# Shared expert units with their low parts on GpSimd, a single-pass table, and a reordered start of Mamba

## The chip, the cores and the metric

The kernel runs on one core of a Trainium2 chip. Time is the device time of one execution in microseconds (us). The engines are TensorE (PE, with its weight loads as PEld), VectorE (DVE), ScalarE (ACT), GpSimd (POOL) and SyncE (SP), which here only issues DMAs.

## The reference

A float32 stack over 4 x 1024 tokens of width 128. Each line normalises x and adds a layer's output:

```python
x = x + 0.5 * moe(layernorm(x))       # 8 experts, 2 per token, one shared
x = x + mamba(layernorm(x))           # forward and reversed selective scan
x = x + 0.5 * moe(layernorm(x))
x = x + 0.5 * ternary_ffn(layernorm(x))
x = x + attention(layernorm(x))       # causal, 16 heads
x = x + 0.5 * ternary_ffn(layernorm(x))
```

The expert layer and the core of the Mamba layer are:

```python
gates = softmax(relu(xf @ Wr1 + br1) @ Wr2 + br2)
tg, ti = top_k(gates, 2); tg = softmax(tg / 2)
out = silu(xf @ Ws1 + bs1) @ Ws2 + bs2
for e in range(8):
    h = silu(xf @ We1[e] + be1[e]) @ We2[e] + be2[e]
    out = out + sum(tg * (ti == e), -1)[:, None] * h
...
h = exp(dt * A) * h + (dt * x) * B_t      # per step, 16 states
y = sum(h * C_t) + x * D
```

## The kernel before, in words

The six layers run one after the other, in program order: experts (3 to 281 us), Mamba (284 to 1310), experts again (about 1316 to 1586), ternary, attention, ternary. The tokens lie in SBUF as x, in 8 blocks of 512 (BLK).

**Matmul precision.** A float32 product is made of three matmuls in the fp32r format: a value is split into a high part (the fp32r copy, by ACT or DVE) and a low part (value minus high), and high x high, low x high and high x low are summed in PSUM. Some matmuls (the table and positions, below) have plain float32 operands.

**Expert layer (`moe_ffn`).** First come norm and router for all eight blocks. Then the work goes in 31 *units*: 8 shared ones (SH, one per block, with the shared weights), then 23 jobs of 512 gathered rows with one expert's weights each. A unit u is: `up` on PE, four chunks k of 128 hidden channels; ACT writes each chunk as raw (Silu, float32) and for k = 0 to 2 again as hh (Silu, fp32r); DVE's `low(u, k)` makes hl = raw - hh, and for k = 3 also hh by a copy; `down` on PE from hh and hl; ACT evicts; PE transposes (`out_T`); DVE's `take` adds the rows to x (shared units) or copies them to yt, which SP stores. raw has one buffer a chunk, hh and hl two.

Beside the shared units DVE carries the routing, in an order written out by hand in its unit loop: `gate_top` ahead of the loop, `gate_second` (second choice, ends with s_M, a copy to spare) after (0, 1), `counts`, `places`, `split_places` (ends with s_dst, another copy to spare) up to (1, 1). PE's `positions` sits between. Then `hot(q)`, q = 0 to 15, each four scaled one-hot tiles `oha` (128x96) and one tile of one-hots `ohb` (128x512, in pool8, which it shares with the normalised rows xn), placed by `GROUPS`; PE multiplies them into a *table* in PSUM (`table`, 64 float32 matmuls), which says what token stands in each of the gathered places. `experts` makes the expert of each job, `indices` (after unit 5) turns the table into gidx. POOL waits for gidx and gathers: `gather(j)` is four indirect DMAs of rows, `weights(j)` one of a job's weights. POOL's order is: power for the gates (tt), weights 0 to 2, gathers 0 to 2, then gather(j + 2), weights(j + 2) for each job. DVE's `weights` (after unit 2) turns tt into the gates wab, which are used in the next layer when the experts' rows are added.

**Mamba (`mamba`).** The scan goes in 16 blocks b of 16 slots v, with a block -1 that only prepares. `uses_of(b)` says which use of the one PSUM tile O lies in which slot: T transposes a chunk's rows, x is half a convolution (12 fp32r matmuls), xp the projection to B, C and dt, dt its second product, z the gate. `silus_of` places ACT's silus. In each slot PE broadcasts a row of B (`rows`), DVE makes a product u x B over 128x1024 (L1645) and two scans (L1621), POOL two products H x C (L1757), and POOL makes dt and u of the next block, 3 to 6 slots after each dt use. Before that, POOL fetches the expert layer's rows back into a ring (`fetch`, one indirect DMA each, 8 a block), ACT weighs them (`weigh`), DVE adds them (`returned`) and takes statistics; `root(n)` on POOL makes the reciprocal root and `normalize` on ACT the rows of a chunk.

## Time and profile before

| | |
|---|---|
| median of 3 runs | 2830.28 us (2826.9 to 2831.55) |
| the profiled execution | 2828.44 us |
| its span | 2826.6 us |
| granted TensorE clock, mean | 0.949 |
| PE busy | 2464.1 us (87%) |
| DVE busy | 2216.3 us (78%) |
| ACT busy | 1698.0 us (60%) |
| POOL busy | 1431.2 us (51%) |

These shares are means over layers with different limits. The slices below (40 equal ones of 70.7 us, busy share in tenths) show the first expert layer in slices 1 to 4, Mamba in 5 to 19, the second expert layer in 20 to 22:

```profile
PE   7998387878888898887899599979999999997999
DVE  7998478989999999998899556458877777755444
POOL 2474688888888888885177460023233323310000
```

In Mamba DVE and POOL are the busiest, in the expert layers PE and DVE.

### The profile page before, as it was taken

What the parts mean: (1) busy time and instruction counts of PE and PEld (TensorE: products, weight loads), DVE (VectorE), ACT (ScalarE), POOL (GpSimd) and SP (SyncE); (2) the same over time, 40 slices, a digit from 0 to 9 for tenths busy, and PEclk for the clock granted to TensorE, in tenths of its full rate; (3) what the DMA queues carried; (4) which work ended last, traced back from release to release, by engine and by line L of the source; (5) the groups of instructions that cost most, each with busy time, mean ns of one, the idle gap of its engine ahead of it and who ended that gap; (6) DMA issues with size and microseconds to landing.
All of it is one profiled execution on the core that took longest, in us unless ns stands there. A gap on an engine that the chain in (4) does not pass through costs nothing. (4 is left out here: it accounts for less than half of the span.)

```text
span 2826.6 us, 35819 instructions
## 1 busy us (share of the span) xinstructions
PE 2464.1 (87%) x10648; PEld 1570.2 (56%) x10648; DVE 2216.3 (78%) x4293; ACT 1698.0 (60%) x2969; POOL 1431.2 (51%) x1482
## 2 busy tenths in 40 slices
PE   7998387878888898887899599979999999997999
PEld 5876243333333344324777378855555555646887
DVE  7998478989999999998899556458877777755444
ACT  3676465556666666652477355535776767764555
POOL 2474688888888888885177460023233323310000
PEclk9999598999999999999999799989999999998999
DMA  2256222222222222222056410000000000001000
GB/s 76 64 163 117 84 68 67 74 69 73 68 75 73 75 75 75 72 78 73 24 129 146 98 49 2 1 16 1 1 1 1 2 1 1 1 1 42 8 8 15
DMA packets 99497, 146.07 MB, mean 52 GB/s; under 512 B 13036, under 2 KB 50540, under 8 KB 99124
## 3 DMA queue, kind: packets, MB, share of 16 engines
q1 hardware_dynamic: 82196, 98.60, 11.7%
q0 software_dynamic: 16608, 44.78, 7.4%
q8 instruction: 83, 1.36, 0.2%
q14 instruction: 98, 0.80, 0.1%
q10 hardware_dynamic: 512, 0.53, 0.1%
HBM read 124.98 MB, written 18.87 MB: 51 GB/s over the span
## 5 line engine op out<-in xcount | busy, mean ns | idle before, releaser
L1757 POOL TENSOR_TENSOR a_hc<-a_H,a_cb 128x512 f32<-128x512 f32 x512 | 619.3, 1231 | 135.1 <-DVE a_H L1621 128.1
L1413 PE MATMUL a_Y<-a_hc,ident 128*128 128x512 f32 x1024 | 539.4, 637 | 54.4 <-POOL a_hc L1757 45.9
L2113 ACT ACTIVATE a_pt<-a_W 128x512 f32<-128x512 f32 (+3 forms) x768 | 345.8, 496 | 201.7 <-PE a_W L2013 198.1
L1539 ACT ACTIVATE a_dA<-a_dt,a_aneg 128x512 f32<-128x512 f32 x512 | 342.6, 714 | 193.9 <-POOL a_dt L1776 103.8
L1413 PEld LDWEIGHTS a_Y<-a_hc,ident 128*128 128x128 f32 x1024 | 183.6, 197 | 306.9 <-POOL a_hc L1757 211.8
L1645 DVE TENSOR_TENSOR a_BX<-a_u,a_BX 128x1024 f32<-128x1024 f32 x256 | 308.4, 1210 | 43.8 <-PE a_BX L1347 22.0
L1621 DVE TENSOR_TENSOR_SCAN a_H<-a_dA,a_H,a_BX 128x512 f32<-128x512 f32 x256 | 312.2, 1262 | 2.5 <-ACT a_dA L1539 2.5
L2336 POOL TENSOR_SCALAR_AFFINE_SELECT a_pt<-a_pt 128x512 f32<-128x512 f32 x128 | 91.3, 713 | 421.9 <-ACT a_pt L2113 421.9
L1621 DVE TENSOR_TENSOR_SCAN a_H<-a_dA,a_BX 128x512 f32<-128x512 f32 x256 | 296.5, 1201 | 1.0 <-POOL a_hc L1757 1.0
L2199 DVE CUSTOM_DVE_ANT_0 a_masked<-a_W,a_mask 128x384 f32<-128x384 f32 (+3 forms) x512 | 231.9, 486 | 78.8 <-PE a_W L2000 76.8
L2013 PE MATMUL a_W<-a_Q,a_K 128*128 128x512 f32 (+3 forms) x768 | 283.8, 385 | 1.7 <-ACT a_pt L2113 1.6
L2000 PE MATMUL a_W<-a_K,a_Q 128*128 128x512 f32 (+3 forms) x768 | 268.6, 364 | 8.5 <-POOL a_K L2345 3.9
L1347 PE MATMUL a_BX<-a_bcs,a_sel 128*128 128x512 f32 x256 | 174.4, 682 | 96.8 <-DVE a_H L1621 82.9
L722 POOL DMA_INDIRECT m_xg<-m_xrows,m_gidx x184 | 190.8, 1037 | 120.9 <-DVE m_didx L606 65.4
L1053 DVE TENSOR_TENSOR t_hl<-t_raw,t_hh 128x512 fp32r<-128x512 f32 x128 | 87.4, 691 | 182.1 <-ACT t_hh L954 182.1
L2013 PEld LDWEIGHTS a_W<-a_Q,a_K 128*128 128x128 f32 x768 | 145.8, 191 | 138.5 <-ACT a_pt L2113 90.2
L2202 DVE TENSOR_REDUCE a_mx<-a_W 128x1 f32<-128x512 f32 x256 | 166.4, 678 | 46.9 <-PE a_W L2000 46.8
L448 ACT ACTIVATE m_raw<-m_U,m_wg 128x512 f32<-128x512 f32 x248 | 173.9, 702 | 45.9 <-PE m_U L336 33.3
L849 PE MATMUL t_U<-t_hh,t_wh 128*128 128x512 f32 x512 | 201.4, 393 | 0.0
L851 PE MATMUL t_U<-t_hl,t_wh 128*128 128x512 f32 x512 | 199.6, 390 | 0.0
L850 PE MATMUL t_U<-t_hh,t_wl 128*128 128x512 f32 x512 | 199.3, 389 | 0.0
L953 ACT ACTIVATE t_raw<-t_U,t_scal 128x512 f32<-128x512 f32 x128 | 88.1, 688 | 166.6 <-PE t_U L851 166.6
(324 smaller groups left out, 5462.8 us busy)
## 6 DMA issues: line engine op xcount, KB each, us to landing
a_cb<-a_crow SPq DMA_DIRECT2D x256, 256.0 KB, 3.3
m_orows<-m_yt SPq DMA_DIRECT2D x46, 256.0 KB, 3.2
t_wst<-ternary_w SPq DMA_DIRECT2D x22, 256.0 KB, 2.7
m_xrows<-m_pool SPq DMA_DIRECT2D x16, 256.0 KB, 2.3
m_xg<-m_xrows,m_gidx POOLq DMA_INDIRECT x184, 3.5
out<-x SPq DMA_DIRECT2D x8, 256.0 KB, 2.3
m_wg<-moe_ws SPq DMA_DIRECT2D x2, 516.0 KB, 4.6
a_hc<-mamba_conv_rows SPq DMA_DIRECT2D x1, 1024.0 KB, 5.1
```

The lines of the kernel that those rows point to most:

```text
L849: pe.matmul(out, wh[:, piece, c], rhs_h, start=start, stop=False)
L850: pe.matmul(out, wl[:, piece, c], rhs_h, start=False, stop=False)
L851: return pe.matmul(out, wh[:, piece, c], rhs_l, start=False, stop=stop)
L1413: pe.matmul(Y[:, h, :], ident[:], hc[:, g % HCRING, :], start=False, stop=v == NS - 1).then_inc(s_y, 1)
L1539: act.activation(dA[:, G % ARING, :], dt[:, b % 2, h, :], ACT.Exp, scale=aneg[:, d, h, v:v + 1]).then_inc(s_dA, 1)
L1621: dve.tensor_tensor_scan(out, a, bb, init, ALU.mult, ALU.add).then_inc(s_scan, 1)
L1645: dve.tensor_tensor(both_banks(Q), u[:, b % 2, :, :], BX[:, row_bank(Q), :].unsqueeze(1).broadcast_to([P, HALF, BLK]), ALU.mult).then_inc( ...
L1757: pool.tensor_tensor(hc[:, G % HCRING, :], H[:, s, span], cb[:, v % RING, :], ALU.mult).then_inc(s_hc, 1)
L2000: pe.matmul(W[:, s % 3, 0:cols], Q[:, g, tile(t)], K[:, g * GH + j, c * BLK:c * BLK + cols], start=True, stop=True).then_inc(s_S, 1)
L2013: pe.matmul(W[:, 3 + u % 3, 0:BLK - r * P], K[:, g * GH + j, tile(kt)], Q[:, g, c * BLK + r * P:(c + 1) * BLK], start=True, stop=True).the ...
L2113: act.activation(pt[:, u % PR, 0:BLK - r * P], W[:, 3 + u % 3, 0:BLK - r * P], ACT.Exp).then_inc(s_exp, 1)
L2199: dve.tensor_tensor_reduce(masked[:, s % 3, 0:cols], W[:, s % 3, 0:cols], mask[:, BLK - cols:], 1.0, LEAST, ALU.add, ALU.max, dst).then_in ...
```

## The change

In the expert layer, POOL makes the low parts of shared units 0 to 5 (`NPL`), and for k = 3 the high part too, with semaphores of their own (s_hp, s_h3); `low_done` says who signals which. The tables' operands are fp32r: oha, the one-hot tiles (now `slots`, five buffers apart from xn), both, and the constants for `positions`, which ACT copies to `sums`. `table` is one fp32r matmul for each of the 64. `GROUPS` starts at (2, 0) instead of (1, 2) and ends at (5, 1); `indices` follows at (6, 1) and is one step and a cast, since the table's values are now stored as token - 2048. Gate scratch tiles are reused. On POOL the order is low parts of units 0 to 4, weights 0 to 2, low parts of unit 5, gathers 0 to 2, then the power for the gates, then the rest; DVE's `weights` moves from unit 2 to unit 10.

In Mamba, chunk 1's transpose and convolution go from block 0 to block -1 (slots 10, 12, 14), its projection and dt to earlier slots of block 0; its silu from slot 4 to 2; ACT weighs ring block 1 at (-1, 3) and normalises chunk 1 at (-1, 8); POOL fetches 12 rows ahead of the first root, then 4, clears H, fetches 4.

```diff
-        pool8 = sb("pool8", [P, 8, BLK])
-        xn = pool8[:, 0:NXN, :]
-        oha = sb("oha", [P, NOA, TPB, HOT])
+        xn = sb("xn", [P, NXN, BLK])
+        slots = sb("slots", [P, NOB, BLK], F32R)
+        oha = sb("oha", [P, NOA, TPB, HOT], F32R)
...
+        both = sb("both", [P, TILES, E], F32R)
+        sums = sb("sums", [P, 2 * P], F32R)
...
-        GROUPS = {(1, 2): (0, 1), (1, 3): (1, 3), (2, 0): (3, 4), (2, 1): (4, 5), (2, 2): (5, 6), (2, 3): (6, 8),
-                  (3, 0): (8, 9), (3, 1): (9, 10), (3, 2): (10, 11), (3, 3): (11, 13),
-                  (4, 0): (13, 14), (4, 1): (14, 15), (4, 2): (15, 16)}
-        TABLE_DONE = 5
+        GROUPS = {(2, 0): (0, 1), (2, 1): (1, 2), (2, 2): (2, 3), (2, 3): (3, 4), (3, 0): (4, 5), (3, 1): (5, 6),
+                  (3, 2): (6, 7), (3, 3): (7, 9), (4, 0): (9, 10), (4, 1): (10, 11), (4, 2): (11, 12),
+                  (4, 3): (12, 14), (5, 0): (14, 15), (5, 1): (15, 16)}
+        TABLE_DONE = (6, 1)
+        NPL = 6
+
+        def low_done(u, k):
+
+            return (s_hp, KC * u + k + 1) if u < NPL else (s_hl, KC * (u - NPL) + k + 1)
         def ohb(q):
-            return pool8[:, (NXN + q) % NOB, :]
+            return slots[:, q % NOB, :]
...
-                        pe.wait_ge(s_hl, KC * u + k + 1)
+                        pe.wait_ge(*low_done(u, k))
...
-                    pe.matmul(T[:, 0:E * TILES], C["tri"], m, start=True, stop=True)
-                    pe.matmul(T[:, E * TILES:], C["ones"], m, start=True, stop=True).then_inc(s_pos, 1)
+                    pe.matmul(T[:, 0:E * TILES], sums[:, 0:P], m, start=True, stop=True)
+                    pe.matmul(T[:, E * TILES:], sums[:, P:], m, start=True, stop=True).then_inc(s_pos, 1)
...
-                pe.wait_ge(s_consts, 16)
+                pe.wait_ge(s_sums, 1)
...
-                        wait(act, s_hl, KC * (u - 1) + k + 1)
+                        if u:
+                            act.wait_ge(*low_done(u - 1, k))
...
+                        act.wait_ge(s_consts, 16)
+                        act.activation(sums[:], cst[:, 0:2 * P], ACT.Copy).then_inc(s_sums, 1)
...
-                    if NOB - NXN <= q < NOB:
-                        dve.wait_ge(s_xst[q - NOB + NXN], 16 * (SH // NXN))
...
-                    val = T[:, 0:COLS]
-                    step(dve.tensor_scalar(g1_[:], val, float(TOKENS) + 0.5, float(TOKENS), ALU.is_ge, ALU.mult))
-                    step(dve.scalar_tensor_tensor(g2_[:], val, -1.0, g1_[:], ALU.add, ALU.subtract))
-                    step(dve.tensor_scalar(gidx[:], g2_[:], 0.0, None, ALU.max))
+                    step(dve.tensor_scalar(gidx[:], T[:, 0:COLS], float(TOKENS // 2), None, ALU.add))
...
-                        if u < UNITS:
+                        if NPL <= u < UNITS:
                             low(u, k)
...
+                        if (u, k) == TABLE_DONE:
+                            indices()
+                    if u == SH + 2:
                         weights()
-                    if u == TABLE_DONE:
-                        indices()
...
+                def low(u, k):
+                    if k < KC - 1:
+                        pool.wait_ge(s_hh, 3 * u + k + 1)
+                        if k == 0:
+                            wait(pool, s_dn, u - 1)
+                    else:
+                        pool.wait_ge(s_raw, KC * (u + 1))
+                        pool.tensor_scalar(hh[:, u % 2, k, :], raw[:, k, :], 1.0, 1.0, ALU.mult, ALU.mult)\
+                            .then_inc(s_h3, 1)
+                        pool.wait_ge(s_h3, u + 1)
+                    pool.tensor_tensor(hl[:, u % 2, k, :], raw[:, k, :], hh[:, u % 2, k, :].bitcast(F32),
+                                       ALU.subtract).then_inc(s_hp, 1)
+
+                for u in range(NPL):
+                    for k in range(KC):
+                        low(u, k)
+                    if u == NPL - 2:
+                        pool.wait_ge(s_ej, 1)
+                        for j in range(NWG - 1):
+                            weights(j)
                 pool.wait_ge(s_consts, 16)
-                pool.wait_ge(s_dd, 1)
-                pool.tensor_tensor(tt[:], root_e[:], dd[:], ALU.pow).then_inc(s_tt, 1)
-                pool.wait_ge(s_ej, 1)
-                for j in range(NWG - 1):
-                    weights(j)
                 pool.wait_ge(s_idx, 1)
                 for i in range(NXN):
                     pool.wait_ge(s_xst[i], 16 * (SH // NXN))
                 for j in range(NXG):
                     gather(j)
+                pool.wait_ge(s_dd, 1)
+                pool.tensor_tensor(tt[:], root_e[:], dd[:], ALU.pow).then_inc(s_tt, 1)
...
-                    7: ("dt", 0, 0), 9: ("dt", 1, 0)}
+                    7: ("dt", 0, 0), 9: ("dt", 1, 0), 10: ("T", 0, 1), 12: ("x", 0, 1), 14: ("x", 1, 1)}
         if b == 0:
-            return {0: ("T", 0, 1), 1: ("x", 0, 1), 2: ("x", 1, 1), 5: ("xp", 0, 1), 6: ("x", 0, 2),
-                    7: ("dt", 0, 1), 8: ("x", 1, 2), 9: ("dt", 1, 1), 10: ("z", 0, 0), 11: ("z", 1, 0),
+            return {3: ("xp", 0, 1), 5: ("dt", 0, 1), 6: ("x", 0, 2), 7: ("dt", 1, 1), 8: ("x", 1, 2),
+                    10: ("z", 0, 0), 11: ("z", 1, 0),
...
-            return {4: (1, None), 12: (2, 0)}
+            return {2: (1, None), 12: (2, 0)}
...
-                        if (b, v) == (-1, 7):
+                        if (b, v) == (-1, 3):
                             back.weigh(act, ring, 1, 0, s_weighed)
                             back.weigh(act, ring, 1, 1, s_weighed)
-                        if (b, v) == (-1, 12):
+                        if (b, v) == (-1, 8):
                             normalize(1)
...
-                fetch(2 * TPB)
+                fetch(2 * TPB + 4)
+                root(0)
+                fetch(4)
                 pool.memset(H[:], 0.0).then_inc(s_cst, 1)
-                root(0)
-                fetch(2 * TPB + 4)
+                fetch(4)
                 root(1)
...
-    val = (np.arange(2)[:, None] * TOKENS + TILE * P).reshape(1, -1) + p + 1
+    val = np.tile(TILE * P, 2)[None] + p - TOKENS // 2
```

## Rows read from the trace of the kernel before

**Rows 1.** Windows by stage: us, each engine's busy time, PEclk, DMA share, GB/s.

```profile
40.00:112.00 72.00, 60.40 (x319) 50.13 (x319) 65.01 (x173) 37.61 (x60) 15.01 (x10) 0.95 0.10 27
112.00:220.00 108.00, 107.45 (x525) 85.58 (x524) 106.31 (x179) 86.88 (x148) 83.26 (x82) 1.00 0.54 142
...
338.00:412.00 74.00, 57.96 (x154) 30.63 (x154) 56.83 (x52) 48.74 (x81) 62.71 (x56) 0.87 0.24 70
```

**Rows 2.** Timeline, 44 to 64 us, DVE: start, length, instruction, [idle before <-releaser].

```profile
49.49 0.15 DVE L535 COPY m_spare<-m_both 128x1 f32<-128x1 f32 x1
...
59.70 0.15 DVE L575 COPY m_spare<-m_dmod 128x1 f32<-128x1 f32 x1
60.37 1.04 DVE L589 TENSOR_SCALAR m_oha<-m_cst,m_dbase 128x96 f32<-128x96 f32 x4
61.32 0.68 DVE L594 TENSOR_TENSOR m_pool<-m_cst,m_dmod 128x512 f32<-128x512 f32 x1
```

**Rows 3.** The same timeline, PE.

```profile
62.06 2.02 PE L389 MATMUL m_T<-m_oha,m_pool 128*128 128x96 f32 x8 [6.43 <-DVE m_pool L594]
```

**Rows 4.** Timeline around 104 us, DVE and then POOL.

```profile
104.38 0.20 DVE L606 CAST m_didx<-m_dest 128x64 uint32<-128x64 f32 x1
...
104.84 0.95 POOL L722 DMA_INDIRECT m_xg<-m_xrows,m_gidx  x1 [32.71 <-DVE m_didx L606]
```

**Rows 5.** Groups by shape, POOL: xcount | busy us, mean ns | idle before.

```profile
L1757 POOL TENSOR_TENSOR a_hc<-a_H,a_cb 128x512 f32<-128x512 f32 x512 | 619.3, 1231 | 135.1 <-DVE a_H L1621 128.1 <-PE a_Y L1413 6.0
...
L104 POOL DMA_INDIRECT a_ring<-m_orows,m_didx x64 | 64.0, 1000 | 14.0 <-issue 11.1 <-POOL a_pads L1716 0.5 <-PE a_Y L1413 0.5
...
L2345 POOL TENSOR_SCALAR a_K<-a_stk,a_heads 128x512 fp32r<-128x512 f32 x128 | 88.1, 704 | 9.2 <-DVE a_stk L2265 9.2
```

**Rows 6.** Timelines at about 298, 435 and 652 us, DVE and POOL.

```profile
298.27 0.69 DVE L122 TENSOR_TENSOR x<-x,a_ring 128x512 f32<-128x512 f32 x1 [1.14 <-ACT a_ring L114]
...
435.27 4.94 DVE L122 TENSOR_TENSOR x<-x,a_ring 128x512 f32<-128x512 f32 x2
...
435.93 2.50 POOL L1757 TENSOR_TENSOR a_hc<-a_H,a_cb 128x512 f32<-128x512 f32 x2
...
438.39 1.26 POOL L1776 TENSOR_TENSOR a_dt<-a_rl,a_um 128x512 f32<-128x512 f32 x1
...
652.69 2.55 DVE L122 TENSOR_TENSOR x<-x,a_ring 128x512 f32<-128x512 f32 x2
...
651.73 2.95 POOL L1757 TENSOR_TENSOR a_hc<-a_H,a_cb 128x512 f32<-128x512 f32 x2 [0.24 <-DVE a_H L1621]
```

**Rows 7.** Expert-stage timelines; DMA issues (us to landing); waits, 112 to 282.

```profile
49.27 5.48 POOL L735 TENSOR_TENSOR m_tt<-m_root_e,m_dd 128x32 f32<-128x32 f32 x1 [16.20 <-DVE m_dd L532]
...
125.85 0.94 POOL L713 DMA_INDIRECT m_wg<-moe_we,m_widx  x1 [0.30 <-issue]
...
132.50 0.46 DVE L639 CAST m_w1h<-m_wg 128x512 fp32r<-128x512 f32 x1
...
m_wg<-moe_we,m_widx POOLq DMA_INDIRECT x46, 4.3
...
DVE m_w1h L639 <- DMA m_wg<-moe_we,m_widx: 5.7, 4, 2.5
```

**Rows 8.** Timeline, DVE, Mamba's first two blocks.

```profile
337.68 2.36 DVE L1645 TENSOR_TENSOR a_BX<-a_u,a_BX 128x1024 f32<-128x1024 f32 x2
...
355.26 1.23 DVE L1645 TENSOR_TENSOR a_BX<-a_u,a_BX 128x1024 f32<-128x1024 f32 x1 [5.69 <-PE a_BX L1347]
...
411.62 2.36 DVE L1645 TENSOR_TENSOR a_BX<-a_u,a_BX 128x1024 f32<-128x1024 f32 x2 [10.87 <-POOL a_u L1770]
```

**Rows 9.** Timelines, PE at 346 us and POOL at 366 us.

```profile
346.26 0.79 PE L1365 MATMUL a_O<-a_xh,a_wch 128*128 128x512 f32 x1 [3.14 <-DVE a_xl L1665]
...
348.99 0.63 PE L1365 MATMUL a_O<-a_xh,a_wch 128*128 128x512 f32 x1
...
366.71 2.20 POOL L1757 TENSOR_TENSOR a_hc<-a_H,a_cb 128x512 f32<-128x512 f32 x2
```

More of the change, by code:

```diff
@@ L174, in moe_ffn @@
             at += n
-        NWG, NXG, NYT, NXN, NOB, NOA = 4, 3, 3, 4, 8, 5
+        NWG, NXG, NYT, NXN, NOB, NOA = 4, 3, 3, 4, 5, 5
         wg = sb("wg", [P, NWG, ROW])
@@ L197, in moe_ffn @@
         g1 = lambda n: sb(n, [P, TILES])
-        sh, ex, gt, eq, cc, oh1, gm, oh2, both, pr1, pr2 = map(g8, (
-            "sh", "ex", "gt", "eq", "cc", "oh1", "gm", "oh2", "both", "pr1", "pr2"))
-        eq2, cc2 = g8("eq2"), g8("cc2")
+        sh, ex, gt, eq, cc, oh1, gm, oh2, pr1, pr2 = map(g8, (
+            "sh", "ex", "gt", "eq", "cc", "oh1", "gm", "oh2", "pr1", "pr2"))
+        both = sb("both", [P, TILES, E], F32R)
+        sums = sb("sums", [P, 2 * P], F32R)
         mx, sm, rs, top1, cm, top2, cm2, dd, tt, t1, w0 = map(g1, (
@@ L211, in moe_ffn @@
         widx = sb("widx", [P, JOBS], U32)
-        g1_, g2_ = (sb(n, [P, COLS]) for n in ("g1", "g2"))
         gidx = sb("gidx", [P, COLS], U32)
@@ L226, in moe_ffn @@
         s_wsh, s_wsl = sem("wsh"), sem("wsl")
+        s_sums = sem("sums")
         s_mv, s_ve, s_rstd, s_xn = sem("mv"), sem("ve"), sem("rstd"), sem("xn")
@@ L233, in moe_ffn @@
         s_up, s_raw, s_hh, s_hl = sem("up"), sem("raw"), sem("hh"), sem("hl")
+        s_hp, s_h3 = sem("hp"), sem("h3")
         s_dn, s_ye, s_yT, s_yo = sem("dn"), sem("ye"), sem("yT"), sem("yo")
@@ L530, in gate_second @@
                     step(dve.scalar_tensor_tensor(gm[:], oh1[:], -2.0, gt[:], ALU.mult, ALU.add))
-                    first_of_equals(gm, top2, eq2, cc2, cm2, oh2)
+                    first_of_equals(gm, top2, eq, cc, cm2, oh2)
                     dve.tensor_tensor(dd[:], top2[:], top1[:], ALU.subtract).then_inc(s_dd, 1)
@@ L534, in gate_second @@
                     ch.join()
-                    dve.tensor_copy(spare[:], both[:, 0, 0:1]).then_inc(s_M, 1)
+                    dve.tensor_copy(spare[:], both[:, 0, 0:1].bitcast(F32)).then_inc(s_M, 1)
                 def weights():
@@ L693, in _ @@
                                 experts()
-                    if u == 2:
+                        if (u, k) == TABLE_DONE:
+                            indices()
+                    if u == SH + 2:
                         weights()
-                    if u == TABLE_DONE:
-                        indices()
             @block.gpsimd
```

## The prediction

> **What bounds the kernel now.** I read the windows by stage first, then the timelines of VectorE (DVE), GpSimd (POOL), TensorE (PE) and ScalarE (ACT) in the three stretches that the diff touches, and last, for prices, the grouped instructions. The diff acts in two expert stages, near 40 and near 1346 us, which in the timeline are copies of each other 1305.7 us apart, and once in the first blocks of Mamba. What lies outside only moves with them.
>
> In the shared part of an expert stage (40 to 112 us) DVE is busy 65.0 of 72 us and POOL 15.0 [rows 1]. DVE carries the router, then the destinations, then sixteen pairs of one-hot tiles, with the low parts of the hidden rows between them. PE idles 6.43 us for the first pair, and starts cold after it [rows 3]. The part ends in a handover: the indices are written at 104.38, POOL's first gather starts at 104.84, and PE transposes the gathered rows some 8 us later [rows 4]. From 112 to 220 us DVE is busy 106.3 of 108 us, and POOL issues without a pause in the same rhythm, 6.65 us for one unit (weights of job 3 issued at 125.85, DVE's cast that is in step with them a unit later at 132.50) [rows 1, 7]. Near its end the stage waits for the gathered weights, 5.7 us in four waits [rows 7]. So what a shorter shared part is worth is the shift of the first gather, and whatever delays POOL behind it comes off again.
>
> In Mamba DVE multiplies and scans. The first product starts at 337.68; then DVE idles 5.69 us before 355.26, since PE is busy with convolution matmuls of the second block, and 10.87 us before 411.62, since POOL hasn't finished that block's u [rows 8].
>
> **Experts: what leaves DVE.** 24 low parts (a DVE operation of this size is 0.69 long and starts the next some 0.60 later) and six casts (0.46 for one) [rows 6, 7] are 17.1 us of DVE per stage, some 14.5 of them ahead of the handover. Without any other effect my step-by-step schedule gives: s_M at 48.4 instead of 49.5, destinations at 56.5 instead of 59.7 [rows 2], then four or five pairs a unit at 1.57 us (1.04 and 0.68 us overlapping a little) [rows 2], which PE (28 matmuls a unit, 60.40 us for 319 [rows 1], so some 5.8 us a unit with the residual rows, and the table between) follows in 7.6 to 8.1 us; gather at 90.3. That is 14.5 us earlier per stage, the upper bound.
>
> **Experts: what POOL takes.** A two-input POOL operation of 128x512 took 1.23 us, a one-input one to fp32r 0.70 [rows 5]; so 4 x 1.23 + 0.70 = 5.6 us a unit. It is shorter than the 7.6 us pace: POOL as such isn't the bound. But the rows show that DVE and POOL hold each other up. DVE's sum of two SBUF tiles takes 0.69 us alone; two of them took 4.94 us while POOL did three two-input operations (435.93 to 439.65) [rows 5, 6], and 2.55 us against two, of which POOL's own second was stretched, 2.95 for both [rows 6]. In the first case DVE waited until POOL paused, in the second they alternated. DVE's work here is of that kind: nine of the twelve steps of the second choice, most of the places, and the one-hot tile of each pair (iota and dmod both in SBUF).
>
> The Trainium skill, page "SBUF — State Buffer", section "Who interferes with whom", says that a VectorE instruction with two SBUF inputs contends with a GpSimd instruction that reads SBUF, and that the second to issue blocks entirely until the first is done. By that rule 14.5 us can't be had; the trace agrees in that 0.69 became 4.2 for one, but it also shows a wait across several operations, which the rule, read as one instruction, doesn't give.
>
> With alternation, step by step: POOL's first low part runs from 44.0 to 45.25, and each two-input step of DVE then waits for the one in progress, about 0.7 us; the second choice ends at 54.0 instead of 49.5. PE has idled 6 us by then and starts cold [rows 3]. Counts, places and split, with POOL in the way until about 58.5, give destinations at 64.6 (59.7 before). From here the pairs run with fewer neighbours: a unit of five pairs and the residual add is 5 x 1.57 + 0.6 = 8.5 us plus 1.2 to 2 us of waits, about 10, where it was 11.5 to 12.3 before. The sixteenth pair is in the table at 99.8. The indices now come one unit later in the order, after out_T of unit 4, so 102.6; the first gather at 102.9. Gain 1.95 us per stage, between -8 (DVE waits for POOL's pauses throughout; see the rivals) and 14.5. I take alternation, since the stretch in which POOL's operands come in one at a time from ACT resembles the second case more.
>
> **Experts: the order on POOL.** The power for the gates, 5.48 us on POOL [rows 7], moves from 49.27, where POOL had nothing else to do, to behind the first twelve gathers. Queued behind it are gather 3, weights 3 and all later ones, with no pause in which to recover. Weights 3 were issued at 125.85, landed 4.3 us later at the median and are cast at 132.50 [rows 7], so 2.3 us of the 5.8 (with the issue) are covered: 3.5 us lost there. At the end, where the weights come last, the whole 5.8 counts, less what POOL catches up. I take 4.3, bounds 0 and 5.8. Its price is the same if the first gather moves, because everything behind it moves along. Weights 0 to 2 go behind the fourth unit's low parts, 3.8 us of issue, hidden since no one needs them before the handover. The table's cheaper passes and the positions' are on PE, which waits for DVE; at nothing, at most a microsecond if DVE weren't last. The new wait for sums on PE and ACT's copy lie 15 us ahead of use; the freed xst waits had been satisfied. Per stage: 1.95 - 4.3 = -2.35, so 4.7 us slower in both.
>
> **Mamba.** Moved ahead of block 0: the transpose and both convolution halves of chunk 1; inside it, the projection from slot 5 to 3 and dt from 7, 9 to 5, 7. Fetches go from 8 + 12 around root(0) to 12 + 4 + 4, so ring 1 is landed at about 312 and is weighed in ACT's gap after its first silu; sums and setup end on DVE at 323.3. But ACT's normalize(1) now stands ahead of dt and waits for root(1) until 324.0. u of block 0 ends at 338.1 (337.6 before). Then PE does 24 convolution matmuls, the first twelve cold (such a run started at 346.26 and its seventh at 348.99, 0.455 us apiece, about 5.3 in all) [rows 9], and the first row broadcasts stand behind them: first product at 342.4 instead of 337.7, 4.7 us late. The 5.69 us and one xl (0.6) are gone from block 0, so by the sixth product DVE is 1.7 to 1.9 ahead. The end of block 0 goes by POOL: from 366.71 [rows 9] it works through v = 5 to 15: 11 pairs of products at 2.46 or less, six fetches at 1.00 [rows 5], eight steps to dt and u and two bcs at 1.26 [rows 6], 45.7 us, so until about 412, which fits DVE's start at 411.62 [rows 8]. Moved two slots earlier, v = 14 and 15 (two pairs of products, a fetch, a bcs: 4.9 + 1.0 + 1.3, 7.3 us with the gap between) no longer lie ahead of u: 7.3 + 1.9 = 9.2 us gained. These 7.3 us remain as POOL's backlog in block 1; it idled 11 us there before. I keep 9.2; bounds 3 and 14 (PE cold for all 24 and backlog paid; POOL not last).
>
> **Sum.** 9.2 - 4.7 = 4.5 us faster against the profiled execution's 2828.4 us (span 2826.6), 2823.9; that execution lies 1.8 under the median of the runs shown, so 2825.8 for a median, rounded to 2826.
>
> **Rivals.** (1) Starvation, slower: DVE waits for POOL's pauses, as in the first of the two cases. Then s_M waits until POOL has run out of units 0 and 1, 58.6; destinations 67.5; a unit of five pairs 12.4 us; first gather 112.8, 8 us later than now. It decides as soon as POOL's next operand is ready before its operation ends in the stretch 44 to 58. For it: ACT delivers a chunk about every 1.2 us (an estimate: two passes of its own a chunk, and PE at 5.8 us for four), POOL needs 1.23. Against: the two stretched pairs. Per stage -8 - 4.3: 24.6 in both, with 9.2 back, 15.4 slower: 2846. (2) Contention light: gather at about 92 to 96; 2 x (10.5 - 4.3) + 9.2 = 21.6 faster: 2809; the full bound, 14.5, gives 2801. For it: between chained steps of DVE there are gaps. Against: both of the overlaps in [rows 6] were stretched. (3) Mamba gives only 3, or the late start costs more, with alternation: 2832.
>
> **Chances.** Alternation 0.38, starvation 0.24, light contention 0.26, weak Mamba 0.12. A measurement of this kernel tells 0.2%, 5.7 us, from no change. Alternation itself straddles that bound on the fast side (4.5 us), so I share it: 0.17 faster, 0.16 same, 0.05 slower. With the rest: faster 0.17 + 0.26 + 0.02 = 0.45; same 0.16 + 0.02 + 0.05 = 0.23; slower 0.05 + 0.22 + 0.05 = 0.32. Range 2802 to 2846; the likeliest case's own is 2818 to 2834.
>
> **What would show it.** In the changed profile: the spare copy behind the second choice near 54 (48.4: no contention; 58.6: starvation); two-input DVE operations of 1 us and more beside POOL's, and whether one ever waits through two; the first gather near 102.9; an idle DVE before the cast of w1h at job 3 of 3 to 4 us; stage end to follow. In Mamba, the first product near 342, no idle before the fourth, and block 1's first near 402. I am wrong if DVE's waits beside POOL are rare, or if DVE is starved.

## The result

The changed kernel takes 2851.82 us (median of 5 runs, 2842.25 to 2854.85) against 2830.28 (2826.9 to 2834.07): 1.0069 times the time before, 95% interval 1.0055 to 1.0083, so 0.7% slower. The forecast was 2826, range 2802 to 2846.

| | before | changed |
|---|---|---|
| profiled execution | 2828.44 us | 2854.85 us |
| its span | 2826.6 us | 2853.1 us |
| DVE busy | 2216.3 us | 2223.4 us |
| POOL busy | 1431.2 us | 1506.3 us |

DVE was to lose 34 us of work (17 a stage), yet its busy time rose by 7: the trace counts an instruction as busy while POOL holds it up (the rows of L599 below). That is the first thing to see. The windows of the changed kernel, same stretches and columns as [rows 1]:

```profile
40.00:112.00 72.00, 53.70 (x224) 42.88 (x223) 64.34 (x129) 32.63 (x53) 40.29 (x33) 0.81 0.07 23
112.00:220.00 108.00, 102.09 (x485) 81.52 (x484) 96.21 (x167) 79.86 (x136) 82.17 (x77) 0.97 0.50 124
```

From 40 to 112 us DVE is busy as long as before with 129 instructions instead of 173, and PE has done 224 matmuls where it had done 319, at a granted clock of 0.81 in the mean. Of the 95 that are missing 66 are no lag: the table and the positions are now one pass each (66 matmuls instead of 132). The other 29 are.

Where the 26.5 us of span lie, from the timelines of both. "Router" is the reduction m_mx on DVE (40.0 us in both), "last tile" the start of the sixteenth one-hot tile, "first gather" POOL's first m_xg, "end" the last job's copy m_yt on DVE, all in us:

| first expert stage | before | changed | later by |
|---|---|---|---|
| router to last tile | 57.3 | 66.2 | 8.9 |
| last tile to first gather | 7.5 | 8.9 | 1.4 |
| first gather to first job's copy | 29.4 | 32.0 | 2.6 |
| first to last job's copy | 146.0 | 149.0 | 3.0 |
| sum: router to end | 240.2 | 256.0 | 15.8 |

The second stage goes from 240.4 to 256.5, 16.1 longer. Mamba gives 6.1 back (end of stage to the start of DVE's last product: 1022.0, now 1015.9), the rest is 0.6 longer: 15.8 + 16.1 - 6.1 + 0.6 = 26.4 (0.1 is lost in rounding).

The timeline of the changed kernel's DVE shows how (start, length, instruction; x4 is four in a row, "..." stands for rows left out):

```profile
39.97 0.42 DVE L530 TENSOR_REDUCE m_mx<-m_T 128x32 f32<-128x256 f32 x1 [3.02 <-PE m_T L320]
...
52.07 0.15 DVE L545 COPY m_spare<-m_both 128x1 f32<-128x1 f32 x1
...
64.29 0.15 DVE L585 COPY m_spare<-m_dmod 128x1 f32<-128x1 f32 x1
64.36 2.90 DVE L599 TENSOR_SCALAR m_oha<-m_cst,m_dbase 128x96 fp32r<-128x96 f32 x4
...
83.90 4.14 DVE L599 TENSOR_SCALAR m_oha<-m_cst,m_dbase 128x96 fp32r<-128x96 f32 x4
87.96 0.68 DVE L602 TENSOR_TENSOR m_slots<-m_cst,m_dmod 128x512 fp32r<-128x512 f32 x1
...
95.11 4.33 DVE L599 TENSOR_SCALAR m_oha<-m_cst,m_dbase 128x96 fp32r<-128x96 f32 x4
...
106.19 0.69 DVE L602 TENSOR_TENSOR m_slots<-m_cst,m_dmod 128x512 fp32r<-128x512 f32 x1
111.07 0.69 DVE L621 TENSOR_TENSOR m_hl<-m_raw,m_hh 128x512 fp32r<-128x512 f32 x1 [4.19 <-ACT m_hh L460]
...
114.13 0.20 DVE L611 CAST m_didx<-m_dest 128x64 uint32<-128x64 f32 x1
```

POOL in the same timeline:

```profile
84.16 3.81 POOL L748 TENSOR_TENSOR m_hl<-m_raw,m_hh 128x512 fp32r<-128x512 f32 x3 [6.37 <-ACT m_hh L460]
...
115.08 1.09 POOL L727 DMA_INDIRECT m_xg<-m_xrows,m_gidx  x1 [13.93 <-DVE m_didx L611]
```

Four small operations take 1.04 us when nobody disturbs them [rows 2]. At 83.90 they take 4.14 us, exactly beside three subtractions of POOL. Over the whole kernel the groups say the same (columns as in [rows 5]); first before, then changed:

```profile
L589 DVE TENSOR_SCALAR m_oha<-m_cst,m_dbase 128x96 f32<-128x96 f32 x128 | 33.6, 326 | 0.0
```

```profile
L748 POOL TENSOR_TENSOR m_hl<-m_raw,m_hh 128x512 fp32r<-128x512 f32 x48 | 65.6, 1386 | 54.4 <-ACT m_hh L460 53.2
...
L599 DVE TENSOR_SCALAR m_oha<-m_cst,m_dbase 128x96 fp32r<-128x96 f32 x128 | 59.1, 524 | 0.0
```

The 128 one-input operations of the tables cost 25.5 us more, 12.8 a stage. The 32 two-input tiles behind them cost nothing: all but one have the length of before (shortest, median and longest in ns):

```profile
L602 DVE TENSOR_TENSOR m_slots<-m_cst,m_dmod x32: 677/680/1136, 67.2 to 1422.3; 128x512 fp32r<-128x512 f32 x32
```

Added up instruction by instruction against the shortest of its kind before, the first stage's DVE operations up to the last tile are 21.4 us longer, 15.8 of it in one-input operations.

### The profile page after: what moved, and what is told of

It is laid out like the page before. It is cut to its first block and busy times, and to the rows that moved or that the text cites. A ratio compares the mean times of both kernels' runs of the same rounds, so it can differ in the third digit from the quotient of the medians.

```text
span 2853.1 us, 35545 instructions
## 1 busy us (share of the span) xinstructions
PE 2465.8 (86%) x10516; PEld 1565.2 (55%) x10516; DVE 2223.4 (78%) x4229; ACT 1698.5 (60%) x2971; POOL 1506.3 (53%) x1542
## 5 line engine op out<-in xcount | busy, mean ns | idle before, releaser
L1369 PE MATMUL a_BX<-a_bcs,a_sel 128*128 128x512 f32 x256 | 174.1, 681 | 85.7 <-DVE a_H L1643 84.1
L1075 DVE TENSOR_TENSOR t_hl<-t_raw,t_hh 128x512 fp32r<-128x512 f32 x128 | 87.5, 691 | 181.7 <-ACT t_hh L976 181.6
L727 POOL DMA_INDIRECT m_xg<-m_xrows,m_gidx x184 | 179.0, 973 | 82.2 <-issue 54.3
L456 ACT ACTIVATE m_raw<-m_U,m_wg 128x512 f32<-128x512 f32 x248 | 174.3, 704 | 44.1 <-PE m_U L343 34.7
## 6 DMA issues: line engine op xcount, KB each, us to landing
a_cb<-a_crow SPq DMA_DIRECT2D x256, 256.0 KB, 3.2
m_orows<-m_yt SPq DMA_DIRECT2D x46, 256.0 KB, 4.7
t_wst<-ternary_w SPq DMA_DIRECT2D x22, 256.0 KB, 2.8
m_xrows<-m_xn SPq DMA_DIRECT2D x16, 256.0 KB, 2.3
out<-x SPq DMA_DIRECT2D x8, 256.0 KB, 2.3
```

## The experiments

Each ratio below is against the kernel before, run beside it. The experiments fall into four sets: A (mamba_alone, pow_back, npl_zero, early_indices), in which the kernel before took 2911.79 us, B (free_pool, probe, table_only, all_good) with 2828.68, C (pow_late, pow_back_2, npl_two, all_good_2) with 2829.24, and D (changed_again, npl_zero_2, all_good_3) with 2901.68. In A and D, the long sets, the part from the first gather to the stage's end was 198 to 209 us instead of 174 to 183 in every kernel. What makes a set long is open: the record has chip number 12 for B and for D. Totals are therefore compared within a set only, and ratios of different sets with care: npl_zero and npl_zero_2 are one kernel, and came to 0.9999 and 0.9959, with intervals that do not overlap. Up to the last tile the changed kernel agrees between a short and a long set within 1.4 us (66.2 and 66.8, 65.9 and 65.4), in Mamba within 0.7; its first gather scatters more (75.1 and 74.8, 71.1 and 74.2), so that a difference of less than 4 us there says little. Numbers from the timelines, in us, first and second stage:

| kernel | router to last tile | router to first gather | first gather to end | end to last product of Mamba |
|---|---|---|---|---|
| before | 57.3, 57.4 | 64.8, 64.9 | 175.4, 175.5 | 1022.0 |
| changed | 66.2, 66.8 | 75.1, 74.8 | 180.9, 181.7 | 1015.9 |
| npl_zero | 59.2, 59.1 | 67.5, 64.9 | 204.5, 207.3 (long set) | 1016.3 |
| npl_two | 59.6, 59.6 | 68.1, 66.9 | 180.9, 181.7 | 1016.0 |
| free_pool | 44.4, 45.4 | 51.4, 52.4 | 182.5, 180.7 | 1014.6 |
| pow_back_2 | 65.8, 65.5 | 74.6, 71.5 | 177.6, 178.0 | 1016.1 |
| table_only | 57.3, 57.4 | 65.5, 65.2 | 174.0, 174.1 | 1021.7 |
| all_good | 57.4, 57.4 | 64.2, 63.3 | 174.3, 173.8 | 1013.1 |
| pow_late | 56.3, 56.3 | 63.1, 64.6 | 181.3, 181.7 | 1013.3 |
| all_good_2 | 57.4, 57.4 | 62.5, 63.8 | 179.5, 177.0 | 1009.3 |

### The probe: which operations hold each other up

Behind the end of the kernel before, eight each of seven kinds of DVE operation, four times: alone, beside POOL subtractions (two SBUF inputs), beside POOL's one-input operation, beside POOL memsets.

```diff
+for part in range(4):                        # DVE; POOL runs 76 or 90 operations beside parts 1 to 3
+    for i in range(8): dve.tensor_scalar(o1[:, i, :], sa[:, 0:96], sc[:, 0:1], sc[:, 1:2], ALU.is_equal, ALU.mult)
+    for i in range(8): dve.tensor_tensor(o2[:, i, :], sa[:], sb_[:], ALU.is_equal)
+    for i in range(8): dve.tensor_tensor(o3[:, i, :], Z[:], sb_[:], ALU.subtract)      # Z in PSUM
+    ...
```

> The kernel before, and behind its end a probe: eight each of seven kinds of DVE operation (one-input with two per-partition scalars from SBUF 128x96; two SBUF inputs 128x512; PSUM and SBUF 128x512; one-input from PSUM 128x96; reduction 128x256; cast 128x512; scalar_tensor_tensor from PSUM and SBUF), first alone, then beside an unbroken row of POOL subtractions 128x512, then beside one-input POOL operations, then beside POOL memsets. Theory A: beside POOL's subtractions the small one-input operation from SBUF takes some 1.25 us instead of 0.26, the two-SBUF-input one 1.2 to 1.9 instead of 0.68, and both sides alternate; those with a PSUM input and the reduction stay as they are. Rival (only operations with two SBUF inputs are held up): the small one stays near 0.26 us. Beside memsets nothing is held up by either.

The windows of the four parts, for the small one-input operation alone (window, its length, busy and count; then clock and DMA):

```profile
2827.40:2851.50 24.10, 2.00 (x8) 0.50 0.00 0
2851.50:2891.10 39.60, 8.88 (x8) 0.50 0.00 0
2951.00:2984.00 33.00, 4.42 (x8) 0.50 0.00 0
3008.80:3036.00 27.20, 2.57 (x8) 0.50 0.00 0
```

And the timeline of DVE beside the subtractions:

```profile
2851.57 8.88 DVE L2483 TENSOR_SCALAR pr_ohts<-pr_sa,pr_sc 128x96 fp32r<-128x96 f32 x8
2860.37 13.46 DVE L2486 TENSOR_TENSOR pr_ohtt<-pr_sa,pr_sbb 128x512 fp32r<-128x512 f32 x8
2873.76 4.86 DVE L2488 TENSOR_TENSOR pr_pstt<-pr_Z,pr_sbb 128x512 fp32r<-128x512 f32 x8
2878.54 2.37 DVE L2490 TENSOR_SCALAR pr_psts<-pr_Z,pr_sc 128x96 fp32r<-128x96 f32 x8
```

| eight on DVE, us | alone | beside subtractions | beside one-input | beside memsets |
|---|---|---|---|---|
| one-input, scalars from SBUF, 128x96 | 2.00 | 8.88 | 4.42 | 2.57 |
| two SBUF inputs, 128x512 | 4.90 | 13.46 | 8.24 | 4.89 |
| PSUM and SBUF, 128x512 | 4.88 | 4.86 | 4.86 | 4.87 |
| one-input from PSUM, 128x96 | 2.38 | 2.37 | 2.37 | 2.37 |
| reduction, 128x256 | 2.71 | 2.70 | 2.70 | 2.70 |
| cast, SBUF, 128x512 | 2.78 | 2.77 | 5.70 | 5.64 |
| scalar_tensor_tensor, PSUM and SBUF | 4.89 | 4.88 | 4.86 | 4.86 |

Theory A holds: from the second on the small operation waits for a whole POOL subtraction every time, 1.22 us apiece instead of 0.24, and the two-input one goes at 1.67 instead of 0.60, in strict turns. Its price is the length of POOL's operation, not of its own. The three kinds with a source in PSUM, and the reduction, are free of it. The expectation on memsets was wrong: they hold up casts, and a little the small one. And the turns aren't always fair: beside the eight casts one POOL subtraction took 3.84 us, and the casts lost nothing. The Trainium skill, page "SBUF — State Buffer", section "Who interferes with whom", lists copies, casts and tensor_scalar among those that can take the pair of ports shared with GpSimd, and tensor_reduce as never doing so. By these rows the trace agrees for tensor_scalar, casts and the reduction (8.88, 5.70 and 2.70 us for eight, 2.00, 2.78 and 2.71 alone); a copy from SBUF was not probed.

### What the change could bring, and what the hold-up costs

free_pool: POOL's parts cut to 8 of 512 columns, which leaves out most of the low parts of the first six shared units.

```diff
-pool.tensor_tensor(hl[:, u % 2, k, :], raw[:, k, :], ...
+pool.tensor_tensor(hl[:, u % 2, k, 0:8], raw[:, k, 0:8], ...
```

> The changed kernel, but POOL's low and high parts of units 0 to 5 are made for 8 of 512 columns only (the rest is zeroed once before), so the shared units' result is not the reference's; all waits and signals stay. Neither DVE nor POOL has the work, which is the bound of what the change could bring. Theory A (contention): destinations at 56 to 58, pairs at 1.57 us each, last pair near 88 and first gather at 91 to 96. Theory B (order): the first gather not before 105. My blind schedule without contention said 90.3.

DVE, then POOL, with the router at 45.1 here (the zeroing of the rest stands ahead of it):

```profile
89.52 0.68 DVE L603 TENSOR_TENSOR m_slots<-m_cst,m_dmod 128x512 fp32r<-128x512 f32 x1
...
95.56 0.20 DVE L612 CAST m_didx<-m_dest 128x64 uint32<-128x64 f32 x1
```

```profile
96.50 1.08 POOL L728 DMA_INDIRECT m_xg<-m_xrows,m_gidx  x1 [8.40 <-DVE m_didx L612]
```

The first gather comes 51.4 us behind the router, 91.4 on the other kernels' base; the schedule without contention said 90.3. So the work taken off DVE was counted rightly. The kernel is only 9.4 us faster than before (2819.31 in one run, before 2828.68), Mamba's 7 included, and two things hide the rest. The experiment's own zeroing, two POOL operations on 128x2048 and two on 128x512 ahead of each router, delays it by 5.1 and 4.9 us, since DVE's normalisation waits there (four one-input operations in 4.85 us instead of 1.08); without it the gain would be about 19 us, an estimate from these two delays. And the stages lose 5 to 7 us behind the first gather.

npl_zero: DVE makes all low parts, all else as changed.

```diff
-        NPL = 6
+        NPL = 0
```

> The changed kernel with NPL = 0: DVE makes all low parts, everything else of the change stays (order of the pairs, place of the indices, fp32r table, the power behind the gathers, Mamba). Theory A (DVE and POOL hold each other up, operation by operation): the destinations are back before 61, the DVE operations have their undisturbed lengths, and the first gather starts at 107 to 110, 5 to 8 us earlier than with POOL's low parts (115.1), although DVE has 17 us more work: 10 to 16 us faster in all than the changed kernel. Theory B (the later first pair and the indices behind unit 6 delay the handover, whoever makes the low parts): first gather at 113 to 116.

DVE, and then POOL:

```profile
99.07 0.68 DVE L602 TENSOR_TENSOR m_slots<-m_cst,m_dmod 128x512 fp32r<-128x512 f32 x1
...
106.44 0.20 DVE L611 CAST m_didx<-m_dest 128x64 uint32<-128x64 f32 x1
```

```profile
107.39 1.00 POOL L727 DMA_INDIRECT m_xg<-m_xrows,m_gidx  x1 [33.70 <-issue]
```

Gather at 107.4, as theory A said; ratio 0.9999 (0.9988 to 1.0010). With 14.8 us more work up to there DVE is 7 us sooner at its last tile. The kernels give the ledger of the first stage up to the last tile: low parts on DVE cost 59.2 - 44.4 = 14.8; low parts on POOL cost DVE 66.2 - 44.4 = 21.8 in waits; the new order costs 59.2 - 57.3 = 1.9. So the change bought 14.8 us for 21.8 and paid 1.9 on top: 8.9. In the second stage it is 13.7 for 21.4, and 1.7 on top: 9.4.

For the total effect within one set, the changed kernel and this one again:

> The changed kernel itself, as the measure for the other two on the same chip: 0.6 to 0.8% slower than before.

> The changed kernel with NPL = 0 once more. If the hold-up between DVE and POOL is the main cause, the handover comes 7 to 8 us earlier per stage than in the changed kernel and the kernel is 14 to 18 us faster than it, 2834 to 2838; what is left over before (4 to 8 us) is the late power and the later indices, less 6 us from Mamba. If the order is the main cause: less than 7 us faster.

changed_again: 1.0021 (1.0012 to 1.0031), npl_zero_2: 0.9959 (0.9944 to 0.9974); 2908.45 and 2890.71 us, 17.7 apart, at the upper end of the 14 to 18 expected. The profiles, in which npl_zero_2 is the slowest of its runs, have 4.7 and 7.3 of that from router to end and 1.8 in Mamba. The rest of both expectations failed: changed_again was to be 0.6 to 0.8% slower than before and is 0.2, and npl_zero_2, expected 4 to 8 us behind before, is 11 ahead of it. So in this set, in which the stages are long behind the first gather, the change as a whole costs less, while the hold-up on DVE up to the last tile is the same (65.9 and 65.4 against 59.2 in both stages). The size of the loss depends on the set; that POOL's low parts cost more than they save does not.

npl_two: POOL makes those of units 0 and 1 alone.

```diff
-        NPL = 6
+        NPL = 2
```

> The changed kernel with NPL = 2: POOL makes the low parts of units 0 and 1 alone, beside the second choice and the destinations, DVE those of all others. From the router's end (the reduction m_mx) to the first gather the kernel with NPL = 0 took 67.5 us, with 6 75.1. If each POOL operation costs DVE a wait of its own whatever DVE is doing, destinations come at about 64 as with 6, the pairs behind run undisturbed, and the distance is 69 to 71. Rival (only the waits beside the one-hot tiles cost something): 66 to 68.

```profile
62.24 0.15 DVE L585 COPY m_spare<-m_dmod 128x1 f32<-128x1 f32 x1
...
62.93 1.04 DVE L599 TENSOR_SCALAR m_oha<-m_cst,m_dbase 128x96 fp32r<-128x96 f32 x4
```

A miss: destinations at 62.2, not 64, first gather 68.1 and 66.9 behind the router: the rival's 66 to 68. The last tile, which scatters less, says it better: 59.6, as with NPL = 0 (59.2), and 6.6 us ahead of the changed kernel. So beside the second choice and the places, POOL's eight subtractions cost DVE in waits about what they save it in work. The loss comes from units 2 to 5: 4.2 us of it between the destinations and the last tile, where the table's small operations stand, and 2.4 ahead of the destinations, where two one-input steps (L582 and L583) took 1.22 us each in the changed kernel and take 0.20 here. One run: 2844.58, before 2829.24.

### The power, and the place of the indices

```diff
                 for j in range(NXG):
                     gather(j)
-                pool.wait_ge(s_dd, 1)
-                pool.tensor_tensor(tt[:], root_e[:], dd[:], ALU.pow).then_inc(s_tt, 1)
```

(and the same two lines in front of the wait for the indices).

> The changed kernel with the power for the gates put between the low parts of unit 5 and the wait for the indices, where POOL idled 13.9 us. If the power ahead of gather 3 delays everything behind it on POOL, each expert stage is 5.5 to 6 us shorter from the first gather to its end and the kernel 11 to 12 us faster than the changed one, about 2840. Rival (the stage behind the first gather is set by PE and DVE, and the power only fills POOL's slack): 0 to 4 us.

> The changed kernel with the power for the gates in POOL's idle time ahead of the indices, once more, for a chip on which the expert stage isn't held up by its transfers. The first gather is where the changed kernel has it; from there to the stage's end 175 to 176 us instead of 180.9 if the power is the whole of the difference; 178 or more if the later place of the indices, at which PE ran out of rows for 3.8 us, has a share.

pow_back came to 1.0016 (1.0000 to 1.0032) in a long set, where its part behind the gather can't be read. pow_back_2: 1.0041 (1.0026 to 1.0057), 2842.51 us; 177.6 and 178.0 from first gather to end, 3.3 and 3.7 less than changed, between the two expectations and next to the second (178 or more). The power isn't the whole of it: some 2.3 us stay. A row of the changed kernel's PE shows from where:

```profile
122.81 1.11 PE L383 MATMUL m_T<-ident,m_xg 128*128 128x128 f32 x4 [3.76 <-DMA m_xg<-m_xrows,m_gidx]
```

Since the indices stand one unit later in the order, PE runs out of shared units while the first rows are fetched. The same wait is in every kernel with the indices at (6, 1) (4.28 us in pow_back_2, 4.14 in npl_two, 3.88 in free_pool), it is 1.91 in early_indices, and before, table_only, all_good and pow_late have none.

The other way round, pow_late puts the late power into the best kernel so far (all_good, below):

> The kernel all_good (before with the table's part and the Mamba part) with one move more: the power for the gates behind the first twelve gathers, and DVE's use of it to unit 10, as in the change. If the 5.5 us on POOL delay everything queued behind, each stage is 5 to 6 us longer from the first gather to its end, in all 10 to 12 us slower than all_good, some 2830. Rival (the weights arrive early enough, only the first 3.5 us show): 3 to 7 us in all.

1.0001 (0.9991 to 1.0010) where all_good had 0.9964 in another short set: by that the move costs 0.37%, 10.5 us in all, as expected. In the profiles it is 5.9 and 9.2 us from router to end, and 7.0 and 7.9 from first gather to end, more than the 5 to 6 expected; a part of that may be the set, since all_good_2, with the power in its old place, is 5.2 and 3.2 us longer there too. Its row on POOL is

```profile
117.81 5.75 POOL L741 TENSOR_TENSOR m_tt<-m_root_e,m_dd 128x32 f32<-128x32 f32 x1
```

early_indices:

```diff
-        TABLE_DONE = (6, 1)
+        TABLE_DONE = (5, 2)
```

> The changed kernel with the indices two hidden chunks after the last pair instead of behind the first chunks of unit 6. The table is complete on PE at about 111.2 and DVE is idle then, so the indices come out some 2.5 us earlier in each expert stage, and the kernel is 4 to 5 us faster than the changed one. Rival (what PE lacks after the handover is not the rows): no change in the end of the stage.

```profile
111.05 0.25 DVE L610 TENSOR_SCALAR m_gidx<-m_T 128x92 uint32<-128x92 f32 x1 [4.30 <-PE m_T L396]
```

The indices come at 111.05 instead of 113.8, as worked out, and DVE now waits for the table. The first gather is 72.4 and 69.0 us behind the router; with the scatter above, that is 2 to 6 us. The ratio, 1.0042 (1.0026 to 1.0057), is from set A, which has no run of the changed kernel, so what it is worth in all stays open.

### Mamba, the table, and a faster kernel

mamba_alone is before with the four Mamba edits of the change.

> The kernel before with only the Mamba part of the change. My step (the reordered start gains) expects the first product 4 to 5 us later after the end of the expert stage, block 1's first product 9 us earlier than before on the same base, and about 6 us left at the end of Mamba, since in the changed kernel's trace 3 of the 9.4 us were given back in block 1: about 2824 us beside 2830, that is 6 us faster. Rival (the gain came from the changed expert stage's end, or is given back entirely): within 2 us of before.

0.9969 (0.9959 to 0.9979), 9 us where 6 were expected. Its stretch from stage end to Mamba's last product is 1015.1, 6.9 less than before's.

table_only is before with the fp32r operands, the single table matmuls, the short indices and the separate tiles.

> The kernel before with only the table's part: fp32r operands, single-pass table and positions, one-step indices, separate one-hot tiles; old places of the pairs and the indices, low parts on DVE, no change in Mamba. DVE sets the handover, and loses only two small steps of the indices (0.5 us or less) and PE some passes: 0 to 2 us faster per expert stage, in all within 0.2% of before. Rival (PE's table passes are on the path): 3 us or more per stage.

0.9991 (0.9982 to 1.0001): 0.7 and 1.1 us a stage, nothing that can be told from no change.

all_good joins both; low parts on DVE, the power and the pairs where they were.

> The kernel before with the table's part and the Mamba part, low parts on DVE and the power in its old place. If the parts add up: 6 us from Mamba and 0 to 4 from the two expert stages, 2820 to 2824 us, the fastest of all. Rival (a shift of the first gather is lost again in the stage): no better than the Mamba part alone.

2819.15 us, 0.9964 (0.9952 to 0.9977): 9.5 us less than the kernel before beside it, and some 33 less than the changed kernel, whose own set had the kernel before within 2 us of this one's. The stages are 238.5 and 237.1 long.

all_good_2 has two edits more:

```diff
-        TABLE_DONE = 5
+        TABLE_DONE = (5, 1)
...
-    10: ("T", 0, 1), 12: ("x", 0, 1), 14: ("x", 1, 1)}
+    10: ("T", 0, 1), 13: ("x", 0, 1)}
...
-            return {3: ("xp", 0, 1),
+            return {0: ("x", 1, 1), 3: ("xp", 0, 1),
```

> The kernel all_good with the indices right behind take(3) at (5, 1) and with the second convolution half of chunk 1 back at slot 0 of Mamba's block 0 (the first half stays ahead of it). The table is complete on PE at 101 and the indices came at 103.3, so 1 to 2 us less per expert stage; in Mamba 12 of the 24 convolution matmuls no longer stand ahead of the first product, 2 to 3 us earlier there, but the later wait may give it back. In all 2 to 5 us faster than all_good. Rival (block 1's start is POOL's in any case): only the 2 us of the stages.

0.9965 (0.9951 to 0.9979), no better than all_good. The Mamba edit brought 3.8 us, 1009.3 from stage end to last product, and kept them; the earlier indices brought the first gather to 62.5 us, and the stage took 3.5 us longer for it. The first job's copy stayed where it was (94.3 us behind the router, 94.1 in all_good, 94.2 before): by then the shared units' own work is last, so in these kernels a first gather ahead of about 65 us buys nothing. And the units of the first stage went at 6.79 us instead of 6.65. POOL's timeline, all_good first and then all_good_2, shows the two rhythms:

```profile
164.50 0.94 POOL L711 DMA_INDIRECT m_wg<-moe_we,m_widx  x1 [0.30 <-issue]
165.75 0.94 POOL L720 DMA_INDIRECT m_xg<-m_xrows,m_gidx  x1 [0.30 <-issue]
167.00 1.35 POOL L720 DMA_INDIRECT m_xg<-m_xrows,m_gidx  x1 [0.30 <-issue]
```

```profile
165.16 1.16 POOL L711 DMA_INDIRECT m_wg<-moe_we,m_widx  x1 [0.63 <-ACT m_ysb L443]
166.63 0.94 POOL L720 DMA_INDIRECT m_xg<-m_xrows,m_gidx  x1 [0.30 <-issue]
```

Five issues at 1.25 us and one stretch of 0.41 make 6.66; with the wait for ACT and a stretched weights gather they make 6.79. The second stage of the same run goes at 6.65, so it is a matter of how the engines fall into step, and which of them holds the pace isn't settled by these runs.

all_good_3 keeps only the Mamba edit of the two:

> The kernel all_good with the second convolution half of chunk 1 back at slot 0 of block 0, indices in their old place. If the earlier indices locked the stage into the slower rhythm, the units go at 6.65 us again and each stage is back at 237 to 239 us from the router's end to the last job, while Mamba keeps the 3.8 us that all_good_2 gained over all_good: 4 us faster than all_good, about 2815. Rival (the rhythm differs from run to run, whatever the edit): 6.8 us may show here too.

0.9953 (0.9939 to 0.9966), the lowest ratio, but from a long set, in which npl_zero_2 has 0.9959 beside it, so it can't be set against all_good's. The jobs alternate there between 6.65 and 8.8 us in this kernel, so the question of the rhythm stays open. Mamba took 1011.0, 4.2 less than the changed kernel in the same set.

## Why the prediction was wrong

**What left DVE: right.** 14.5 us ahead of the handover; free_pool and npl_zero give 14.8 and, in the second stage, 13.7. The gather without contention was to come at 90.3 and would have at 91.4.

**Up to the destinations: the place right, in part by luck.** Foretold were the second choice at 54.0 and the destinations at 64.6; they came at 52.1 and 64.3. The first was 1.9 us sooner: the prediction counts nine steps of twelve with two inputs in SBUF, but the kernel's second choice has nine steps, six of them such. The second took up most of that, since two one-input steps (L582, L583) cost 1.22 us each instead of 0.20, the same omission as in the pairs. Alternation was the rule, with one exception in the second stage, where one small operation waited through three subtractions of POOL (DVE first, the second of its four alone 4.48 us; then POOL):

```profile
1410.00 5.54 DVE L599 TENSOR_SCALAR m_oha<-m_cst,m_dbase 128x96 fp32r<-128x96 f32 x4
```

```profile
1410.93 3.71 POOL L748 TENSOR_TENSOR m_hl<-m_raw,m_hh 128x512 fp32r<-128x512 f32 x3
```

So starvation occurred, but once in both stages; everywhere else up to the last tiles no operation of DVE waited through two. What decides between the two, no run shows.

**The pairs: the step that failed.** I gave a unit of five pairs 1.2 to 2 us of waits, since of a pair only the one-hot tile has two inputs in SBUF, and had the table done at 99.8. The last tile came at 106.2. The waits were in the four small one-input operations ahead of it, which I had taken for free: 12.8 us a stage in the groups, against some 6 in my sum. The two-input tile, to which I had put them, was as long as before (0.680 us in the median). The section of the Trainium skill that the prediction cites, "Who interferes with whom" on page "SBUF — State Buffer", names tensor_scalar as well, and I had used only its line on two inputs; the trace agrees with both lines. Nor did I price what alternation means for a short operation: it pays POOL's 1.22 us for its own 0.24. In the trace of before the tables' operations stood beside nothing on POOL but three weights gathers (there four took 1.18 and 1.08 us instead of 1.04 in the first stage), so their cost was unknown and should have been bounded from above: POOL's 30 operations a stage, 24 at 1.23 and six at 0.70 us, 34 us in all, cost DVE about as much at most when they alternate. It was 21.8.

**From the table to the gather: mis-sized.** 3.1 us foretold, 8.9 from last tile to gather measured (7.5 before). I had let DVE alone set it. PE ended the table at 111.3, 5 us behind the last tile: from 95 to 102 us it had been busy for 2.3 of 7, and from 104 to 108 its granted clock was 0.50, the lower of its two levels (1.2 GHz), and back at 1.00 from 108.4. The indices stand behind two chunks of unit 6, for which DVE waited 4.19 us; early_indices, without them, still has DVE wait 4.30 us, now for PE's table. What of the 5.8 us too little each is worth, these runs don't part. Together with the pairs (6.7 us too little from destinations to last tile, 0.3 of it made up ahead of them) that is the 12.2 us by which the first gather missed 102.9.

**Behind the first gather.** The power was taken at 4.3 a stage, and taking it back from the changed kernel gained 3.8 and 7.0 from router to end: about right (3.3 of the 7.0 lie ahead of the first gather, where the kernels scatter as much). What I left out is that PE runs out of rows once (3.76 us). And the premise "what a shorter shared part is worth is the shift of the first gather" was too simple: it holds for a later one, while all_good_2 gained nothing by an earlier one than before's; only free_pool, whose shared units end sooner too, had its first job earlier (83.8 us behind the router instead of 94.2).

**Mamba: right to half a microsecond at both points foretold, then mis-sized.** In the changed kernel (DVE, timeline):

```profile
357.75 2.36 DVE L1667 TENSOR_TENSOR a_BX<-a_u,a_BX 128x1024 f32<-128x1024 f32 x2 [4.65 <-PE a_BX L1369]
...
417.99 1.22 DVE L1667 TENSOR_TENSOR a_BX<-a_u,a_BX 128x1024 f32<-128x1024 f32 x1
```

Less the 15.8 us by which the stage ended later, these are 342.0 (foretold 342.4) and 402.2 (402.4). But POOL's backlog of 7.3 us, which I had hidden in 11 us of idle time, seems to have surfaced. The waits of block 1, before (411 to 480 us) and then changed (418 to 490; us in total, times, longest):

```profile
PE a_Y L1413 <- POOL a_hc L1757: 7.2, 4, 3.5
...
DVE a_BX L1645 <- PE a_BX L1347: 2.5, 2, 1.5
```

```profile
PE a_Y L1435 <- POOL a_hc L1780: 9.7, 6, 3.5
...
DVE a_BX L1667 <- PE a_BX L1369: 5.7, 3, 2.8
```

DVE waits 3.2 us more for PE's row broadcasts, and PE 2.5 more for POOL's products. In PE's order the broadcasts stand behind matmuls that take these products, so the second is the likely cause of the first, and 3.2 is about what 9.4 lost on its way to 6.1; no run takes the backlog away to show it.

**The rivals.** None was it. Starvation came near in time (2846), by luck: its waits came once, not throughout. In light contention I had argued with the gaps between DVE's chained steps; the pairs have none.

The sum by stage (the first), foretold and measured: -1.95 and +10.3 at the first gather, +4.3 and +5.5 behind it, and once Mamba, -9.2 and -6.1.

## What to carry to other kernels

Before work goes to GpSimd, list every VectorE instruction that will stand beside it by where its operands lie: with its sources in SBUF (two inputs, or a plain one-input operation or a cast) it can wait for a whole GpSimd operation; with a source in PSUM, or as a reduction, it was free in the probe. When the two alternate there is one wait for each GpSimd operation that finds such an instruction beside it, so count both sides, take the smaller number and multiply by GpSimd's duration: here 30 operations a stage, 34 us at most, 21.8 measured. Two stretches of this kernel (435.27 before, 1410.00 changed) went beyond alternation. Work of 0.6 us that keeps GpSimd busy for 1.25 pays only beside instructions of the second kind or beside few long ones. Give the parts of a change back one by one: here one part (Mamba) was worth 6 to 9 us and was hidden under a loss of 32.

## What the runs showed that I had not expected

A POOL memset, which reads nothing, doubled the time of DVE's casts (2.78 us for eight, 5.64 beside it) and left two-input operations alone (4.90 and 4.89). Beside eight casts one POOL subtraction took 3.84 us instead of 1.26: there the one-sided case, the other way round. Indirect DMA issues on POOL vary as well: in the first expert stage of all_good, 19 of the 107 from 110 to 270 us took 1.35 us or more instead of 0.94, 17 of them beside the copy m_yt out of PSUM, two beside the addition to x, and none beside one of DVE's casts. For the one at 167.00 above:

```profile
167.45 0.68 DVE L626 COPY m_yt<-m_R 128x512 f32<-128x512 f32 x1
```

That this copy is the cause isn't shown. A stage whose first gather came 1.7 us sooner was left in a rhythm of 6.79 instead of 6.65 us a unit. And sets differ: the kernel before took 2828.68 us in one and 2911.79 in another. In the profile of its Mamba variant in the latter, 34 and 28 us of that lie in the expert stages behind the first gather and 21 behind the second stage; its Mamba is within 1 us of the changed kernel's (1015.1 and 1015.9). Why is open.
